# A mixture of experts, three of its eight batches dispatched to tiles of 128 rows

## The chip, the cores and the metric

One core of a Trainium2 chip runs the whole program. The metric is the device time of one execution in microseconds, from the median of several runs.

## The reference, cut to what matters

Four layers follow one another: a delta-rule attention, a mixture of 8 experts with capacity, a gated linear attention with a small two-layer block after it, and last a mixture of 16 experts on tokens with 128 channels, of which each token uses the four most probable. The change is in the last two. With `x` the 4096 tokens (8 batches of 512), the last layer is

```
p = softmax(x @ router_w + router_b)            # 16 experts
w, ids = top_k(p, 4);  w = w / sum(w)
y = sum over k of  w[k] * (gelu(x @ w1[ids[k]] + b1[ids[k]]) @ w2[ids[k]] + b2[ids[k]])
out = x_before + y                              # 128 -> 256 -> 128 channels per expert
```

A token needs 4 of 16 experts. The kernel before computes all 16 for every token, with coefficient 0 for the 12 others.

## The kernel before, in words

All state lies in SBUF. `resid` holds the 4096 tokens as 32 tiles of 128 tokens by 128 channels; `scratch`, cut in blocks of 1024 columns by `carve`, and A1 to A7 hold everything else. The five engines each have one program, written out by hand, and meet by semaphores that count steps (`S(name)`, `at(n)`).

The last mixture runs over units: one unit is one expert on one batch of 512 tokens, 8 x 16 = 128 of them. To be as exact as fp32 with fp16 operands, weights and activations are split into a high and a low fp16 part and three products are added (`PARTS`). A unit goes like this:

- TensorE, `hidden1` (2357): for each of two halves of the 256 hidden channels three matmuls, 128 weights columns wide, over 512 tokens, into one of four PSUM banks. It runs three units ahead (`AHEAD`, 2355).
- ScalarE, `all_experts` (1185): a Gelu per half from PSUM to `h_full` (1191), then one copy to fp16, `h_high` (1195).
- GpSimd (745): the low half, `h_low` = `h_full` - `h_high`, 128 x 1024. TensorE's second layer waits for it (`m1_low`).
- TensorE, `outputs1` (2367): for each of four tiles of 128 tokens six matmuls of 128 columns into bank 4 or 5; it waits for `m1_acc` of two units before.
- VectorE, `accumulate` (1851): four operations, `resid` += coefficient x PSUM (1857).

Beside the units of one batch, the small block and the router of the next batch are worked off in pieces at fixed places of the units' count: normalisation (1738), a transpose, two hidden layers (2280) and an output layer (2296) in split fp16 (in fp32 for batch 0), with VectorE making the low parts (1745, 1750), the addition to `resid` (1755), a second normalisation (1768), a transpose, router logits, softmax and the largest four (1780, 1789), and the coefficients (1803). All these products go through one PSUM bank, bank 6. At the end of each batch the coefficients are transposed (2380) and multiplied with the experts' second biases. GpSimd also makes the low parts of the expert weights (722) and adds terms to `resid` (728). Batches 1 to 6 are run from a loop on TensorE (batches 0 to 6 there) and ScalarE, and written out on VectorE and GpSimd. SP writes each finished batch out.

The second layer of the first mixture in this kernel already scatters rows by indirect DMAs issued from GpSimd (655, 672) and reads them back by DMAs issued from SP (512, 522, 527), combined on VectorE at 1572.

## Time and profile before

| what | us |
|---|---|
| median of 3 runs | 923.57 |
| all three runs | 925.18, 923.51, 923.57 |
| the profiled execution's span, first to last instruction | 921.2 |
| TensorE matmul busy in it | 775.8 (84%), 6152 matmuls |
| VectorE, ScalarE, GpSimd busy in it | 693.3, 628.6, 628.8 |
| mean granted TensorE clock | 0.959 |

The profile is of one execution, and its times are from that execution's first instruction. The last mixture is in it from about 537 us to the end. A matmul's length contains its way through the array, so several overlap; what one costs in a row of them is the distance of the starts. PEld is the load of a matmul's stationary operand, which overlaps the matmuls. In order of time a line merges several instructions of a kind, gives the start and the length from the first start to the last end, and in brackets how long the engine had stood idle and what released it.

### The profile page before, as it was taken

To read this page: it belongs to the slowest core of one execution; us is meant where nothing else is said; L and a number is where in the kernel's file an instruction comes from. 1 tells how busy PE (TensorE), PEld (TensorE's weight loads), DVE (VectorE), ACT (ScalarE), POOL (GpSimd) and SP (SyncE) were. 2 spreads that over 40 slices of the span, in tenths; PEclk is the share of its full clock that TensorE was granted. 3 is DMA by queue.
4 is the path that set the end of the run, shared out by engine and by line. 5 is a ranking of instruction groups with operands and counts; after the bars stand their busy time and mean duration, and the time that the engine had idled before them with its cause. 6 is when DMAs were issued, how large, how long until landed. Compare 5 with 4: busy or idle time off the path is not lost.

```text
span 921.2 us, 18395 instructions
## 1 busy us (share of the span) xinstructions
PE 775.8 (84%) x6152; PEld 470.1 (51%) x6152; DVE 693.3 (75%) x2078; ACT 628.6 (68%) x938; POOL 628.8 (68%) x414
## 2 busy tenths in 40 slices
PE   4965765568998789378778989999999999999997
PEld 1343221124453357223233756777677777677775
DVE  7769799994777578598899878766666666666664
ACT  3855233323455567259788988898888888889895
POOL 4008899730477727466888997686868686868695
PEclk9987889999999799769999999999999999999999
DMA  5999300007200030252600000000000000000000
GB/s 149 119 121 207 113 0 0 15 6 194 87 21 7 4 103 25 82 147 50 202 1 1 1 2 2 12 1 11 0 11 0 12 0 0 11 0 11 0 13 13
DMA packets 52792, 40.47 MB, mean 44 GB/s; under 512 B 6059, under 2 KB 44734, under 8 KB 52734
## 3 DMA queue, kind: packets, MB, share of 16 engines
q1 hardware_dynamic: 49662, 37.28, 18.5%
q0 software_dynamic: 3072, 2.51, 1.0%
q8 instruction: 24, 0.39, 0.2%
q14 instruction: 34, 0.28, 0.1%
HBM read 18.07 MB, written 14.88 MB: 36 GB/s over the span
## 4 chain that ended last, share of the span: by engine, by line
POOL 24%; PE 19%; issue 14%; DVE 14%; ACT 6%; DMA 1%; POOLq 0%; DVEq 0%; ACTq 0%; SPq 0%
POOL scratch L745 21%; PE PS L1909 17%; DVE scratch L1670 2%; DVE resid L1572 2%; DVE stats L1407 1%; DVE scratch L1678 1%; POOL resid L731 1%; PE PS L1916 1%; POOL disp L655 1%; ACT scratch L1195 1%; ACT scratch L1191 1%; DVE resid L1420 1%; DVE A L1432 1%; DVE scratch L1410 1%; ACT A L1126 1%
## 5 line engine op out<-in xcount | busy, mean ns | idle before, releaser
L745 POOL TENSOR_TENSOR scratch<-scratch 128x1024 f16<-128x1024 f32 x128 | 272.9, 2134 | 84.5 <-ACT scratch L1195 82.4
L1857 DVE SCALAR_TENSOR_TENSOR resid<-PS,coef,resid 128x128 f32<-128x128 f32 x512 | 144.0, 344 | 108.9 <-PE PS L1909 103.6
L1909 PEld LDWEIGHTS PS<-A,scratch 128*128 128x128 f16 x3456 | 203.4, 98 | 37.8 <-POOL scratch L745 4.8
L1909 PE MATMUL PS<-A,scratch 128*128 128x128 f16 x3456 | 217.1, 219 | 3.9 <-POOL scratch L745 1.6
L1909 PE MATMUL PS<-A 128*128 (+1 forms) x768 | 186.8, 379 | 0.8 <-DVE A L1701 0.2
L1191 ACT ACTIVATE scratch<-PS,cols 128x512 f32<-128x512 f32 x256 | 163.8, 683 | 25.8 <-PE PS L1909 18.9
L1195 ACT ACTIVATE scratch<-scratch 128x1024 f16<-128x1024 f32 x128 | 135.3, 1057 | 5.0
L1909 PE MATMUL PS<-scratch,ident 128*128 128x512 f32 x160 | 88.3, 673 | 52.9 <-DVE scratch L1373 52.9
L614 POOL TENSOR_TENSOR scratch<-A 128x1024 f32<-128x1024 f32 x32 | 76.0, 2383 | 73.8 <-DVE A L1342 56.5
L1909 PEld LDWEIGHTS PS<-A 128*128 128x128 f16 x768 | 70.7, 98 | 66.6 <-issue 0.6
L655 POOL DMA_INDIRECT disp<-A,scratch x64 | 62.9, 982 | 36.5 <-issue 30.2
L1909 PEld LDWEIGHTS PS<-scratch,ident 128*128 128x128 f32 x160 | 30.7, 209 | 100.2 <-DVE scratch L1373 78.1
L1364 DVE TENSOR_TENSOR_SCAN PS<-PS,scratch 128x512 f32<-128x512 f32 x64 | 74.9, 1215 | 1.9
L1909 PE MATMUL PS<-scratch,A 128*128 128x512 f16 (+1 forms) x216 | 52.8, 390 | 1.4 <-DVE scratch L1520 0.7
L672 POOL DMA_INDIRECT y_rows<-A x32 | 34.2, 1070 | 27.6 <-DVE A L1535 23.6
L1916 PE MATMUL PS<-ident,scratch 128*128 128x128 f32 x128 | 21.4, 294 | 33.4 <-ACT scratch L981 15.5
L694 POOL TENSOR_TENSOR scratch<-scratch,A 128x1024 f32<-128x1024 f32 x16 | 38.3, 2394 | 13.1 <-DVE scratch L1670 4.9
L1909 PE MATMUL PS<-scratch,w_r 128*8 128x512 f32 (+1 forms) x106 | 40.2, 509 | 5.9 <-DVE scratch L1753 3.0
L838 ACT ACTIVATE PS<-A 128x512 f32<-128x512 f32 x33 | 19.7, 599 | 35.8 <-DVE PS L1364 35.8
L683 POOL TENSOR_SCALAR A<-resid,scratch 128x128 f32<-128x128 f32 x32 | 31.3, 989 | 18.5 <-DVE scratch L1584 18.5
L838 ACT ACTIVATE PS<-scratch 128x512 f32<-128x512 f32 x31 | 18.6, 601 | 36.6 <-DVE PS L1364 35.5
L1670 DVE TENSOR_TENSOR_SCAN scratch<-PS,scratch 128x512 f32<-128x512 f32 x32 | 37.3, 1206 | 3.1 <-POOL scratch L694 1.2
(336 smaller groups left out, 1330.9 us busy)
## 6 DMA issues: line engine op xcount, KB each, us to landing
A<-A SPq DMA_DIRECT2D x22, 256.0 KB, 7.4
y_rows<-zeros SPq DMA_DIRECT2D x8, 512.0 KB, 6.0
A<-y_rows SPq DMA_DIRECT2D x14, 256.0 KB, 3.5
disp<-zeros SPq DMA_DIRECT2D x4, 528.0 KB, 21.1
resid<-in_L_attn_x SPq DMA_DIRECT2D x8, 256.0 KB, 4.0
A<-scratch SPq DMA_DIRECT2D x8, 256.0 KB, 6.6
A<-in_L_ffn_ew SPq DMA_DIRECT2D x1, 2048.0 KB, 12.3
A<-scratch SPq DMA_DIRECT2D x32, 64.0 KB, 2.0
```

What stands on the lines that cost most here:

```text
L614: pool.tensor_tensor(c_ring[n % 3], bkR[:, 2 * p:2 * p + 2, :], vR[:, i, :].unsqueeze(1).to_broadcast([128, 2, T]), MUL).then_inc(S("r0_c" ...
L655: pool.indirect_dma_start(out=disp[:, :], in_=rows5[RING_OF[b]][:, k, t, :], in_offset=None, out_offset=bass.IndirectOffsetOnAxis(ap=slot_ ...
L672: pool.indirect_dma_start(out=y_rows[:, :], in_=eo[:, ex * NT + t, :], in_offset=None, out_offset=bass.IndirectOffsetOnAxis(ap=xd[:, ex * ...
L694: pool.tensor_tensor(cbuf[n % 2], cs[n % 2], v1[:, bts(b, T)].unsqueeze(1).to_broadcast([128, 2, T]), MUL).then_inc(S("r_c"), 1)
L745: pool.tensor_tensor(h_low[n % 4], h_full[n % 2], h_high[n % 4], SUB).then_inc(S("m1_low"), 1)
L838: A_(bank(n % 2), kk_pair(a, m)[:, max(i, j) % 2, :], ACT.Identity, scale=-1.0, bias=1.0).then_inc(S("r0_decay"), 1)
L1191: A_(h_full[e % 2][:, h * T:(h + 1) * T], bank((e * HC1 + h) % 4), ACT.Gelu, scale=1.0 / SCALE, bias=cols[:, MB1 + e * HC1 + h:MB1 + e * H ...
L1195: A_(h_high[e % 4], h_full[e % 2], ACT.Copy).then_inc(S("m1_high"), 1)
L1364: V.tensor_tensor_scan(out=bank(2 + 2 * (n % 2) + u), data0=bank(u), data1=c_ring[n % 3][:, u, :], initial=0.0, op0=MUL, op1=ADD).then_inc ...
L1670: last = V.tensor_tensor_scan(out=state[:, j, :], data0=bank(2 + j), data1=cbuf[n % 2][:, j, :], initial=0.0, op0=MUL, op1=ADD)
L1857: last = STT(out=resid[:, g, :], in0=bank(4 + e % 2)[:, t * C:(t + 1) * C], scalar=coef[b % 2][:, t, e:e + 1], in1=resid[:, g, :], op0=MUL ...
L1909: return nc.tensor.matmul(o, l, r, start=start, stop=stop)
```

## The change

Batches 0, 1, 3, 6 and 7 are computed as before, 80 units in all. Batches 2, 4 and 5 are dispatched: each token's row is written four times to a DRAM tensor `disp12`, at the next free place of the region of each of its four experts, and then the regions are worked off in tiles of 128 rows that belong to one expert. Four tiles make a group, which goes through the same steps as a unit. There are always 16 groups: 6144 rows and up to 127 of padding for each expert are at most 63 tiles. In parts:

- The order of units becomes a list: 58 dense units, then eight times one dense unit and two groups, then 14 dense units; 96 in all. Nothing of it is a loop any more.
- The small block and router of the batches start at units `CHAIN_AT` (-2, 6, 13, 20, 27, 31, 44 for batches 1 to 7), alternately in PSUM banks 6 and 7, and the block itself is in fp32, without the split. Small operands of VectorE that lay in bank 7 now lie in SBUF.
- For a dispatched batch: SP copies the row three times, VectorE makes fp16 parts, counts and places, TensorE counts by eight small matmuls, GpSimd issues 16 indirect DMAs (48 in all), and its router logits are in fp32.
- After batch 5 VectorE makes a list of tiles (16 or so small operations), TensorE transposes it, and VectorE writes it as integers to SBUF; SP clears 128 rows behind the last one of each expert (16 DMAs at addresses from registers).
- For each group SP loads four weight addresses to registers and issues four DMAs that copy the experts' first-layer weights (both fp16 parts, 128 x 512 each) from SBUF to a ring of four buffers; it loads four row addresses and issues four DMAs of 128 rows of 528 bytes from `disp12` to a ring of seven. TensorE transposes the rows five units ahead, ScalarE copies them to SBUF.
- The first layer of a group is 32 matmuls of 128 columns (for each half and tile one of 48 rows for the bias and three of 128), the second 28 (one for the bias and six per tile), of which 24 take their weights at a register's address. TensorE loads these registers, four at a time, 16 times, behind dense hidden layers.
- VectorE scales a group's output to a ring of four buffers; GpSimd issues four indirect DMAs that scatter it to DRAM `y12`. At the end SP reads `y12` back in 12 DMAs of 256 KB, and VectorE adds the three batches to `resid`, 16 operations each, after the last three dense units.
- 51 of the 96 low halves are made by VectorE instead of GpSimd: all of the group stretch (units 58 to 85), every other one in units 26 to 54, and a few more.

The core of the diff:

```diff
+        DENSE, SPARSE = (0, 1, 3, 6, 7), (2, 4, 5)
+        CHAIN_AT = (None, -2, 6, 13, 20, 27, 31, 44)
+        GT = 4
+        FIRST_DENSE, LAST_DENSE, COMBINE_BEHIND = 58, 8, 5
+        GROUPS12 = -(-((NS * T * TOP1 + E1 * 127) // 128) // GT)
+        left = [("dense", i, e) for i in range(ND) for e in range(E1)]
+        UNITS = [left.pop(0) for _ in range(FIRST_DENSE)]
+        for g in range(GROUPS12):
+            if g % 2 == 0 and len(left) > LAST_DENSE:
+                UNITS.append(left.pop(0))
+            UNITS.append(("group", g, 0))
+        UNITS += left
+        AHEAD, TR_AHEAD, SCATTER_BEHIND = 3, 5, 3
+        XT_RING, YO_RING, XG_RING = 7, 4, 3
+        SCATTER_AT = [CHAIN_AT[b] + 20 for b in SPARSE]
+        LOW_BY_DVE = set(SCATTERS) | {a + 1 for a in CHAIN_AT[2:]} | set(range(SCATTER_AT[NS - 1], SCATTER_AT[NS - 1] + 8))
+        LOW_BY_DVE |= set(range(UNIT_OF_GROUP[0] - 1, UNIT_OF_GROUP[-1] + 5))
...
+            for g in range(GROUPS12):
+                if g >= XT_RING:
+                    n = g - XT_RING
+                    sp.wait_ge(*since(s_yo[n % YO_RING], 16 * GT * (n // YO_RING + 1)))
+                if g >= WT_RING:
+                    sp.wait_ge(S("m1_hid_mm"), at(2 * UNIT_OF_GROUP[g - WT_RING] + 1))
+                columns = registers(mybir.EngineType.SP, tile_list[:, GT * g:GT * g + GT], (E1 - 1) * HC1 * 128)
+                for t, w in enumerate(columns):
+                    sp.dma_start(wt[g % WT_RING][:, t, :, :], w1_hl[:, :, bass.ds(w, HC1 * 128)]).then_inc(s_xt[g % XT_RING][0], 16)
+                first_row = registers(mybir.EngineType.SP, tile_list[:, 128 + GT * g:128 + GT * g + GT], NOBODY)
+                for t, r in enumerate(first_row):
+                    sp.dma_start(xt[g % XT_RING][:, t, :], disp12[bass.ds(r, 128), :]).then_inc(s_xt[g % XT_RING][0], 16)
...
+            def scatter_outputs(g):
+                pool.wait_ge(S("m1_acc"), at(UNIT_OF_GROUP[g]))
+                pool.wait_ge(*since(s_xt[g % XT_RING], 32 * GT * (g // XT_RING + 1)))
+                for t in range(GT):
+                    pool.indirect_dma_start(out=y12[:, :], in_=yo[g % YO_RING][:, t, :], in_offset=None,
...
+            def evict(u, g):
+                dve.wait_ge(S("m1_out_mm"), at(u))
+                if g >= YO_RING:
+                    dve.wait_ge(*since(s_yo[g % YO_RING], 16 * GT * (g // YO_RING)))
+                TS(yo[g % YO_RING], bank(4 + u % 2).rearrange("p (n c) -> p n c", c=C), 1.0 / SCALE, None,
+                   MUL).then_inc(S("m1_acc"), 1)
+            def low_half(u):
+                dve.wait_ge(S("m1_high"), at(u))
+                dve.wait_ge(S("m1_out_mm"), at(u, 4))
+                TT(h_low[u % 4], h_full[u % 2], h_high[u % 4], SUB).then_inc(S("m1_low_dve"), 1)
...
+            for u in range(NU):
+                kind, i, e = UNITS[u]
+                if u + 2 < NU and not LOW_BY_POOL[u + 2]:
+                    low_half(u + 2)
+                if kind == "dense":
+                    accumulate(u, i, e)
+                else:
+                    evict(u, i)
...
             def hidden11(c, h):
-                for k, (sw, sx) in enumerate(PARTS):
-                    last = mm(bank(6), tile(u1_hl[:, sw, :], h), hT11_hl[:, sx, :], start=k == 0, stop=k == len(PARTS) - 1)
+                pe.wait_ge(S("xT_copied"), 3 * B + at(c))
+                chain_bank_read(c)
+                mm(chain_bank(c), tile(u_1, h), hT11).then_inc(S("hid11_mm"), 1)
...
+                for h in range(HC1):
+                    pe.wait_ge(S("m1_hid"), at(2 * u + h, 4))
+                    for t in range(GT):
+                        out = tile(bank((2 * u + h) % 4), t)
+                        mm(out, mb1_hl[:, h * 128:h * 128 + 128], picked_expert(i, t), stop=False)
+                        for k, (sw, sx) in enumerate(PARTS):
+                            last = mm(out, wt[i % WT_RING][:, t, sw, h * 128:h * 128 + 128], tile(x, sx * GT + t), start=False,
+                                      stop=k == len(PARTS) - 1)
...
+                        mm(out, picked_expert(i, t), mb2_hl, stop=False)
+                        for h in range(HC1):
+                            for k, (sw, sh) in enumerate(PARTS):
+                                part = (h_high, h_low)[sh][u % 4][:, h * T + t * 128:h * T + t * 128 + 128]
+                                last = mm(out, part, w2_hl[:, sw, bass.ds(weights_at[i][t] + h * 128, 128)], start=False,
+                                          stop=k == len(PARTS) - 1 and h == HC1 - 1)
...
-            with pe.Fori(0, B - 1) as b:
-                all_experts(b, False)
-            all_experts(B - 1, True)
+            for u in range(NU):
+                if u + AHEAD < NU:
+                    hidden1(u + AHEAD)
+                outputs1(u)
...
+                if u == LIST_AT:
+                    list_transposed()
+                if u + TR_AHEAD < NU and UNITS[u + TR_AHEAD][0] == "group":
+                    group_transposed(UNITS[u + TR_AHEAD][1])
```

## Rows read from the trace of the kernel before

**Rows 1.** The page: TensorE in 40 slices; line 745's group (busy, mean ns, idle)

```profile
PE   4965765568998789378778989999999999999997
...
L745 POOL TENSOR_TENSOR scratch<-scratch 128x1024 f16<-128x1024 f32 x128 | 272.9, 2134 | 84.5 <-ACT scratch L1195 82.4
```

**Rows 2.** Stretches of a whole batch and of the last: busy us by engine

```profile
692.00:740.00 48.00, 47.64 (x545) 34.69 (x543) 33.06 (x130) 42.60 (x58) 36.73 (x19) 1.00 0.02 6
...
870.00:912.00 42.00, 42.00 (x488) 30.88 (x486) 23.05 (x94) 38.54 (x51) 33.17 (x16) 1.00 0.03 8
```

**Rows 3.** TensorE in order of time, last batch (start us, length us)

```profile
875.87 1.46 PE L1909 MATMUL PS<-A 128*128 128x512 f16 x6
...
877.16 1.50 PE L1909 MATMUL PS<-A,scratch 128*128 128x128 f16 x24
...
907.49 1.46 PE L1909 MATMUL PS<-A 128*128 128x512 f16 x6
```

**Rows 4.** TensorE in order of time, a batch run from the loop

```profile
675.17 0.50 PE L1909 MATMUL PS<-coef,A 128*128 128x16 f16 x12
...
675.74 1.46 PE L1909 MATMUL PS<-A 128*128 x6
...
681.54 0.40 PE L1909 MATMUL PS<-coef,scratch 48*128 48x128 f16 x4
...
681.87 1.47 PE L1909 MATMUL PS<-A 128*128 x6
...
699.41 0.82 PE L1909 MATMUL PS<-scratch,w_r 128*128 128x512 f16 x3 [0.32 <-DVE scratch L1753]
...
705.41 0.28 PE L1909 MATMUL PS<-w_v,scratch 128*128 128x128 f16 x2
...
706.76 1.46 PE L1909 MATMUL PS<-A 128*128 x6
...
723.01 0.52 PE L1909 MATMUL PS<-coef,A 128*128 128x16 f16 x12
```

**Rows 5.** TensorE in order of time, the fp32 block of batch 0

```profile
515.88 1.12 PE L1909 MATMUL PS<-scratch,u 128*128 128x512 f32 x2
...
516.84 1.05 PE L1909 MATMUL PS<-u_o,A 128*128 128x128 f32 x8
...
519.68 2.05 PE L1909 MATMUL PS<-u,scratch 128*128 128x128 f32 x16
...
521.57 1.06 PE L1909 MATMUL PS<-ident,scratch 128*128 128x128 f32 x8
...
528.49 0.46 PE L1909 MATMUL PS<-coef,A 128*128 128x16 f16 x12 [0.90 <-DVE A L1774]
```

**Rows 6.** TensorE in order of time, a wait for the splits of batch 1

```profile
561.97 0.28 PE L1909 MATMUL PS<-w_v,scratch 128*128 128x128 f16 x2 [1.08 <-DVE scratch L1753]
```

**Rows 7.** ScalarE in order of time: the step from TensorE's end

```profile
710.24 1.33 ACT L1191 ACTIVATE scratch<-PS,cols 128x512 f32<-128x512 f32 x2 [0.21 <-PE PS L1909]
```

**Rows 8.** VectorE in order of time: single operations

```profile
387.80 2.44 DVE L1572 SCALAR_TENSOR_TENSOR resid<-A,scratch,resid 128x128 f32<-128x128 f32 x8 [6.96 <-DMA A<-y_rows]
...
507.25 1.22 DVE L1678 TENSOR_TENSOR scratch<-PS,scratch 128x1024 f32<-128x1024 f32 x1
...
697.94 0.69 DVE L1752 CAST scratch<-PS 128x512 f16<-128x512 f32 x1 [0.32 <-ACT PS L1138]
...
915.41 1.12 DVE L1857 SCALAR_TENSOR_TENSOR resid<-PS,coef,resid 128x128 f32<-128x128 f32 x4
```

**Rows 9.** GpSimd in order of time: an indirect DMA

```profile
381.55 0.97 POOL L672 DMA_INDIRECT y_rows<-A  x1 [0.30 <-issue]
```

**Rows 10.** SP's queue in order of time: issues of 128 and 256 KB

```profile
385.09 1.90 SPq L522 DMA_DIRECT2D A<-y_rows  x4
...
387.03 5.03 SPq L527 DMA_DIRECT2D A<-y_rows  x6
```

**Rows 11.** The page's DMA issues: KB each, median us to landing

```profile
A<-scratch SPq DMA_DIRECT2D x32, 64.0 KB, 2.0
```

More of the change, by code:

```diff
@@ L348, in build, with chain_bank, low_made @@
+        carry12, region12 = sm[:, 480:496], sm[:, 496:512]
+        def chain_bank(c):
+            return bank(6 + c % 2)
+        def low_made(u):
+            n = sum(p == LOW_BY_POOL[u] for p in LOW_BY_POOL[:u])
+            return (S("m1_low"), at(n)) if LOW_BY_POOL[u] else after("m1_low_dve", n)
         h_full = [carve(n) for n in range(2)]
@@ L409, in build, with registers @@
         fetched = [v[:, :].rearrange("p (n c) -> p n c", c=C) for v in (A6, A7)]
+        def registers(engine, values, most):
+            return nc.values_load_multi_w_load_instructions(
+                values, engines=[engine], min_val=0, max_val=most,
+                skip_runtime_bounds_check_because="made on VectorE from counts that add up to the rows")[1]
         block = ctx.enter_context(nc.Block())
@@ new lines, in _ @@
+            copy_rows(0)
+            written_out(DENSE[0], LAST_UNIT[0])
+            copy_rows(1)
+            written_out(DENSE[1], LAST_UNIT[1])
+            copy_rows(2)
+            sp.wait_ge(*after("tiles_listed", 0))
+            for k in range(E1 // 4):
+                first_free = registers(mybir.EngineType.SP, tail_row[:, 4 * k:4 * k + 4], NOBODY - 128)
+                for r in first_free:
+                    sp.dma_start(disp12[bass.ds(r, 128), :], zeros[:, :]).then_inc(s_tail[0], 16)
@@ L546, in _ @@
+            written_out(DENSE[4], LAST_UNIT[4])
+            for i in range(NS):
+                sp.wait_ge(*after("y_combined", i))
+                sp.dma_start(ov[SPARSE[i]], resid[:, bts(SPARSE[i], NT), :]).then_inc(s_out, 16)
             sp.wait_ge(s_out, X_LAST + 16 * B)
@@ new lines, in _ @@
+            for u in range(NU):
+                if LOW_BY_POOL[u]:
+                    low_half(u)
+                if u in (1, 2):
+                    low_weights(B - 3 + u)
+                for c in range(2, B):
+                    if u == CHAIN_AT[c]:
+                        add_up(c)
+                for i in range(NS):
+                    if u == max(SCATTER_AT[i] - 10, 3):
+                        token_ids(i)
+                for i, n in SCATTERS.get(u, ()):
+                    scatter_tokens(i, n)
+                if u >= SCATTER_BEHIND and UNITS[u - SCATTER_BEHIND][0] == "group":
+                    scatter_outputs(UNITS[u - SCATTER_BEHIND][1])
@@ L1903, in _ @@
+            for i in range(max(0, LAST_DENSE - COMBINE_BEHIND), NS):
+                combine12(i)
             dve.drain().then_inc(stage_done, 1)
@@ L2318, in logits12 @@
             def logits12(c):
-                pe.wait_ge(S("x_low"), at(c))
+                if c in SPARSE:
+                    pe.wait_ge(*after("xT12_copied", sparse_of(c)))
+                else:
+                    pe.wait_ge(S("x_low"), at(dense_of(c)))
+                chain_bank_read(c)
                 for t in range(NT):
+                    logits = chain_bank(c)[:, t * E1:(t + 1) * E1]
+                    if c in SPARSE:
+                        last = mm(logits, tile(A3[:, bts(c, T)], t), u_r[:, :])
+                        continue
@@ L2352, in _ @@
             pe.wait_ge(S("w_low"), at(1))
[L2355 to L2364 removed]
+            weights_at = {}
@@ L2374, in outputs1 @@
                             w = slice((e * HC1 + h) * 128, (e * HC1 + h) * 128 + 128)
-                            part = (h_high, h_low)[sh][e % 4][:, h * T + t * 128:h * T + t * 128 + 128]
-                            last = mm(tile(bank(4 + e % 2), t), part, w2_hl[:, sw, w],
-                                      start=k == 0 and h == 0, stop=k == len(PARTS) - 1 and h == HC1 - 1)
+                            part = (h_high, h_low)[sh][u % 4][:, h * T + t * 128:h * T + t * 128 + 128]
+                            last = mm(out, part, w2_hl[:, sw, w], start=k == 0 and h == 0,
+                                      stop=k == len(PARTS) - 1 and h == HC1 - 1)
@@ L2418, in _, with list_transposed @@
+            def list_transposed():
+                pe.wait_ge(*after("tile_values", 0))
+                chain_bank_read(0)
+                for k in range(2):
+                    mm(bank(6)[0:1, 128 * k:128 * k + 128], tile_values[:, k:k + 1], ident[:, :])
+                last = mm(bank(6)[0:3 * E1, 256:384], tile_expert, ident[:, :])
+                last.then_inc(S("tiles_mm"), 1)
+                read_by[0] = after("tiles_listed", 0)
+            hidden1(0)
             project1(5)
-            hidden1(0, 1)
+            hidden1(1)
```

666 lines of the change are left out of this document (447 added, 219 removed).

## The prediction, made before the changed kernel was run

> **What bounds the kernel now.** I read the page first, then the stretches of the last mixture, then TensorE's order of time in it. The page [rows 1] shows where it is: from the 23rd slice on TensorE is busy 9 tenths at full clock and hardly any DMA runs. The stretch of one whole batch, and that of the last one [rows 2], separate the engines: TensorE 47.64 of 48 us and 42.00 of 42, ScalarE 42.60 and 38.54, GpSimd 36.73, VectorE 33.06. The chain of waits names GpSimd's line 745 most, but GpSimd idles 84.5 us before those 128 steps [rows 1], so TensorE decides. Its order of time in the last batch [rows 3] gives the unit that I count in: one expert on one batch is six matmuls of 512 columns (1.29 us) and 24 of 128 columns (1.34 us), 2.635 us in all (12 units from 875.87 to 907.49; six matmuls from 875.87 to 877.16). Batches 1 to 6 run from the loop at the same pace, so unrolling it is worth nothing. The block before the mixture for the next batch takes what 16 units leave of the 47.84 us from a batch's router matmuls to the next one's (675.17 to 723.01), 5.7 us, with one wait of 0.32 for VectorE's splitting [rows 4].
>
> **Part 1, dense units removed.** 128 units become 80: 48 x 2.635 = **-126.5 us**.
>
> **Part 2, groups added.** 3 x 512 x 4 rows plus the padding bound are 63 tiles, so 16 groups of four, whatever the routing is. A group is 32 first-layer and 28 second-layer matmuls and 8 transposes, all of 128 columns. Rows 3 give 1.34 / 24 = 0.0558 us for a weight load and matmul of that size; 68 x 0.0558 = 3.79. Twelve of them have 48 rows; the four 48-row ones of today take 0.33 us [rows 4], 0.083 each, so +0.33. That is 4.12 x 16 = **+66 us**. A register in an address costs nearly nothing: the 12 small router matmuls, addressed by the loop's register, take 0.57 us from 675.17 to 675.74 [rows 4] against 0.46 busy for those of batch 0 [rows 5], under 10 ns each.
> The Trainium skill, "TensorE: Matmul & The Clock Gate", section "Back-to-back issue gap", says that a sustained stream of weight load and 128-column matmul runs at about 81 ns each. By that 68 would take 5.5 us; this trace has 55.8 ns for the stream, and I follow the trace.
>
> **Part 3, the block before the mixture, fp32.** Its two hidden layers go from three 512-column fp16 matmuls, 0.65, to one fp32 one, 0.96 us each (515.88 to 516.84), its output layer from 1.35 (705.41 to 706.76) to 1.89 (519.68 to 521.57) [rows 4, 5]: 1.16 more, x7 = 8.1. Sparse batches lose the coefficients' transposes and the bias product (0.66) and gain the counts (8 tiny matmuls, about 0.4); their router logits, 4 fp32 matmuls of 16 columns for 12 fp16 ones, I leave at 0.57. With the list of tiles: **+8.5**. The waits for the splits go: 0.32 x 6 [rows 4], and two of 1.08 beside batch 0, one shown [rows 6], of which some come back as a wait for batch 2's normalisation: **-3**.
> TensorE's own work thus falls by 52 us. The rest is what this newly meets.
>
> **Part 4, VectorE in units 26 to 47.** The chains of batches 4, 5, 6 start 7, 7 and 4 units apart instead of 16, and VectorE takes 13 of these 22 units' low halves. Today it has no such row; the nearest of its own is 1.22 us for 128x1024 from PSUM and SBUF [rows 8], the farthest is GpSimd's 2.13 for the same work [rows 1]. I take 1.22, the same engine's, with bounds 0.7 (a 512-column fp16 write takes 0.69 [rows 8]) and 2.13. VectorE: accumulations 22 x 1.05, low halves 13 x 1.22, three chains and a third of 13.2 each, tile list 3.6 (some 17 small dependent operations of 0.2): 86. The 13.2: of the 33.06 busy us of a batch [rows 2] 16 x 1.12 are accumulations, five splits of 0.7 go, 11.7 are left, and gaps between dependent operations and the placing of rows add 1.5. TensorE: 22 x 2.635 + 3.3 x 5.5 = 76. The surplus lands in TensorE's waits for `m1_low_dve`, `m1_acc` and the tile list: **+10** (4 with the slack of two units, 23 with low halves of 2.13).
>
> **Part 5, the first group.** GpSimd has 26 scatters left after unit 43; each takes 0.97 + 0.30 [rows 9], 33 us, then 2.0 to land [rows 11]. Only then may SP load registers, issue 8 DMAs at 0.475 (four in 1.90) [rows 10] and have them land in 2.0: 42 to 43 us. TensorE needs the rows at the end of unit 54, 39 us of its own work later, up to 5 more by part 4. **+4** (0 to 10).
>
> **Part 6, register loads.** On TensorE 16 loads of four values, two at a time, stand in the queue between hidden and output layers, and both layers wait behind them. No row shows one. Below: nothing, if the six matmuls queued ahead (1.3 us) cover a pair. Above: 2.0 us, the landing of a small DMA [rows 11], 32 us in all. I take the nearest round trip in rows, the 0.2 us from TensorE's end to ScalarE's start [rows 7], times four, 0.8 us; with a third covered, **+8** (0 to 32).
> The Trainium skill, "DMA: Bandwidth & Descriptors", section "Latency and other measured facts", states a floor of about 600 ns for a tensor load; 16 of them would be 9.6 us. No run here shows one yet.
>
> **Part 7, supply of the groups.** SP per group: 8 issues x 0.475 + 2 loads x 0.8 = 5.4 us. GpSimd: 4 scatters, 5.1. TensorE: (2.635 + 2 x 4.12)/2 + its loads, about 6. Bytes: 0.5 MB weights, 0.26 MB rows, 0.26 MB out, 1.03 MB; six transfers of 256 KB were issued in 5.03 us [rows 10], 305 GB/s, so 3.4 us. ScalarE: two units and copies about 3.3. All fit under 6, with little room; the seven-deep row ring closes on itself (fetch 8, five units 18, output and evict 5, scatter and landing 7 = 38 us, 5.4 per group). **+4** (0 to 35, below). GpSimd is free of low halves there, so a late scatter harms SP's wait alone, and through it the next rows.
>
> **Part 8, the end.** Three combinations of 16 operations each, 1.04 per four in a row (as accumulations from PSUM; eight of the kind took 2.44 with a wait between [rows 8]), 4.2 each, stand in VectorE's queue after units 93, 94 and 95. Those units have no hidden layer left, so TensorE ends 2.7 after unit 93; VectorE needs 3 x 1.05 + 12.6. It ends 13 after TensorE instead of with one accumulation of 1.12 [rows 8]: **+12**. Their rows are in SBUF by then, scattered 14 dense units earlier. The last write out is of the same size as now. The 3 extra loads at the start (under 0.5 each on SP) and the smaller set-up are covered by loads and products not on the path: 0, at worst 1.4.
>
> **Sum.** -126.5 + 66 + 8.5 - 3 + 10 + 4 + 8 + 4 + 12 = -17. The profiled execution's span is 921.2; the median of the runs is 923.57, 2.4 above it, which I keep. 921.2 - 17 + 2.4 = **906.6 us**.
>
> **Rivals.**
> *Supply-bound groups (slower).* Place: SP's loop over groups, with rings of 7, 4 and 4 behind it. For: `y_rows` transfers issued with a full queue took 0.84 each over six [rows 10]. With 0.84, SP needs 8.3 us per group, 2.3 over TensorE's 6 for 15 groups: +35, **941**. It decides from 7.1 us per group, reached also if one load of four takes 1.65 us. Against: those six were twice to four times larger. Chance 0.2, times from 925 up.
> *No overlap of load and matmul.* If in groups, where 48-row and 128-row operands alternate, every pair took the 0.083 of today's 48-row ones [rows 4], 16 x 56 x 0.027 = +24: 931. All dense rows speak against. Chance 0.03.
> The sentence of the Trainium skill on 81 ns ("TensorE: Matmul & The Clock Gate", above) describes this case.
> *VectorE at GpSimd's pace.* Low halves of 2.13: +13, **920**, as SBUF reads of both fp32 operands could be slower than PSUM's. Chance 0.1.
> *Cheap extras.* Register loads covered, the surplus absorbed, supply in time: -8 - 6 - 4 - 2 = **887**. For it: TensorE's queue had no gap in 30 us of rows 3. Chance 0.25.
> *It does not shrink the work*, if routing filled more tiles: excluded, the count of groups is fixed in the code.
> *Forecast*, 898 to 918: chance 0.42.
>
> **Chances and range.** A measurement of this kernel can tell about 0.2%, 1.8 us. Faster: forecast 0.42, cheap 0.25, most of the VectorE case 0.05: 0.72. Within 0.2%: 0.05. Slower: 0.23. The likeliest sign's own range is 886 to 920; to hold 8 in 10 the top takes in most of the supply case: 886 to 938.
>
> **What would show it.** Dense units at 2.635 and groups at 4.1 on TensorE's order of time; waits of TensorE for VectorE's low half and accumulation around 650 to 720; one wait of some us for the first rows; gaps after every third dense hidden layer by register loads; SP's issues in groups of 5 to 6 us; VectorE alone for 13 us at the end. The forecast is wrong if group units are spaced 7 us or more, if the waits for `xt` recur for each group, or if VectorE's low half is near 2 us.

## The result, and the profile of the changed kernel

The changed kernel takes 993.34 us (988.68 to 994.37) against 923.57 before: ratio 1.0735, interval 1.0697 to 1.0774. The forecast was 906.6, range 886 to 938. The profiled execution has a span of 992.6 us at a mean granted clock of 0.922 (before 921.2 at 0.959). Each ratio below is to the kernel before measured beside that kernel; it took 923.6 to 924.9 us, but twice 945.9 and 951.9, and a time from beside those two is compared with no other.

The page, the lines that answer to [rows 1]: the span, TensorE in 40 slices, and the low halves on GpSimd (45 instead of 128).

```profile
span 992.6 us, 17478 instructions
...
PE   5866555689997892887788679779786969999993
...
L899 POOL TENSOR_TENSOR scratch<-scratch 128x1024 f16<-128x1024 f32 x45 | 97.9, 2179 | 88.2 <-ACT scratch L1403 87.5
```

From the 22nd slice to the 33rd TensorE has no run of nines any more, in the very stretch in which it was to have work without gaps. What it waits for from 530 us on (waits of TensorE: us in total, times, longest):

```profile
PE PS L2238 <- DVE scratch L1957: 19.3, 7, 5.9
PE PS L2231 <- DVE resid L2123: 14.2, 8, 5.3
PE PS L2774 <- DMA A<-disp: 8.8, 2, 8.4
```

Line 1957 is the normalisation ahead of a chain, 2123 the accumulation. An accumulation takes no longer than before (1.13 us for four), so the question is what stood ahead of it in VectorE's queue, which is worked off in order. VectorE in order of time (start us, length us) ahead of the 5.3 us wait for line 2123:

```profile
563.04 2.12 DVE L1948 TENSOR_SCALAR scratch<-scratch 128x8 f32<-128x8 f32 x1
565.19 0.17 DVE L1949 TENSOR_SCALAR scratch<-scratch 128x8 int32<-128x8 int32 x1
565.40 0.17 DVE L1951 TENSOR_TENSOR scratch<-scratch 128x8 f32<-128x8 f32 x1
565.60 2.08 DVE L1952 TENSOR_TENSOR scratch<-scratch 128x8 f32<-128x8 f32 x1
567.71 0.17 DVE L1953 SCALAR_TENSOR_TENSOR scratch<-scratch 128x8 f32<-128x8 f32 x1
```

GpSimd in order of time beside it:

```profile
563.00 2.12 POOL L899 TENSOR_TENSOR scratch<-scratch 128x1024 f16<-128x1024 f32 x1
565.52 4.37 POOL L899 TENSOR_TENSOR scratch<-scratch 128x1024 f16<-128x1024 f32 x2 [0.40 <-ACT scratch L1403]
```

Operations on 4 or 8 numbers per partition take 2.1 us, and they end with GpSimd's: 563.04 + 2.12 = 565.16, and GpSimd's ends at 563.00 + 2.12 = 565.12. Between two of GpSimd's operations they take 0.17. The diff's one line `P7 = carve(8)[:, 0:512]` moved these operands from a PSUM bank to SBUF. This is the first cause (tested below). The first second-layer block of the mixture comes at 557.92 instead of 537.34, before any dense unit is saved.

The second cause is in the groups. TensorE in order of time, one quarter of a hidden bank and one of an output bank:

```profile
844.31 0.23 PE L2231 MATMUL PS<-nr,mb_hl 48*128 48x128 f16 x1
844.47 0.34 PE L2231 MATMUL PS<-A 128*128 128x128 f16 x3
844.74 0.23 PE L2231 MATMUL PS<-nr,mb_hl 48*128 48x128 f16 x1
...
847.94 0.23 PE L2231 MATMUL PS<-coef,nr 48*128 48x128 f16 x1
848.10 0.51 PE L2231 MATMUL PS<-A,scratch 128*128 x6
848.54 0.23 PE L2231 MATMUL PS<-coef,nr 48*128 48x128 f16 x1
```

From start to start a bias matmul of 48 rows and three of 128 take 0.435 us, four of 128 rows would take 0.223 [rows 3]; one and six take 0.60 instead of 0.39. With eight of the first, four of the second and the transposes, 0.45 to 0.54, a group takes 6.4 us, not 4.12.

A wait costs more than its length. In the 4 us behind the wait of 5.34 that ends at 574.07 the granted clock is 0.50, the lower of TensorE's two levels, 1.2 GHz, and 24 matmuls of 128 columns take 2.51 us (574.07 to 576.58) instead of 1.34; the six matmuls of 512 columns behind them take 2.17 (576.58 to 578.75) instead of 1.29, so this wait costs another 2.05 us. 4 us later the clock is 0.98. Windows of all engines (us; busy us of PE, PEld, DVE, ACT, POOL; granted clock; DMA share, GB/s):

```profile
574.00:578.00 4.00, 3.93 (x28) 3.14 (x29) 3.90 (x20) 0.00 (x0) 1.27 (x1) 0.50 0.01 4
578.00:586.00 8.00, 8.00 (x83) 6.06 (x82) 7.48 (x41) 4.76 (x6) 0.73 (x1) 0.98 0.00 0
```

### The profile page after: what moved, and what is told of

Its sections match the earlier page's. It is cut to its first block and busy times, and to the rows that moved or that the text cites. A ratio compares the mean times of both kernels' runs of the same rounds, so it can differ in the third digit from the quotient of the medians.

```text
span 992.6 us, 17478 instructions
## 1 busy us (share of the span) xinstructions
PE 780.5 (79%) x5724; PEld 462.6 (47%) x5724; DVE 743.0 (75%) x1998; ACT 570.4 (57%) x856; POOL 583.3 (59%) x445
## 5 line engine op out<-in xcount | busy, mean ns | idle before, releaser
L2231 PE MATMUL PS<-A,scratch 128*128 128x128 f16 (+1 forms) x2688 | 182.3, 223 | 16.5 <-DVE resid L2123 14.2
L2231 PEld LDWEIGHTS PS<-A,scratch 128*128 128x128 f16 x2688 | 161.5, 100 | 44.9 <-issue 21.3
L2231 PE MATMUL PS<-A 128*128 128x512 f16 (+1 forms) x864 | 169.3, 322 | 0.1
L899 POOL TENSOR_TENSOR scratch<-scratch 128x1024 f16<-128x1024 f32 x45 | 97.9, 2179 | 88.2 <-ACT scratch L1403 87.5
L2123 DVE SCALAR_TENSOR_TENSOR resid<-PS,coef,resid 128x128 f32<-128x128 f32 x320 | 89.9, 343 | 73.7 <-PE PS L2231 67.9
L1396 ACT ACTIVATE scratch<-PS,cols 128x512 f32<-128x512 f32 x160 | 101.7, 685 | 67.1 <-DVE scratch L2137 35.4
L810 POOL DMA_INDIRECT disp<-A,scratch x64 | 62.9, 982 | 36.7 <-issue 30.3
L913 POOL DMA_INDIRECT disp<-A,scratch x48 | 57.7, 1203 | 20.5 <-issue 12.1
L921 POOL DMA_INDIRECT y<-scratch,A x32 | 35.7, 1116 | 50.3 <-DVE scratch L2131 43.0
L2137 DVE TENSOR_TENSOR scratch<-scratch 128x1024 f16<-128x1024 f32 x51 | 62.1, 1218 | 0.3
L921 POOL DMA_INDIRECT y<-A x32 | 36.6, 1145 | 22.3 <-DVE A L2131 13.5
L2238 PEld LDWEIGHTS PS<-ident,scratch 128*128 128x128 f32 x128 | 16.6, 160 | 68.5 <-issue 42.8
```

The lines of the kernel that those rows point to most:

```text
L810: pool.indirect_dma_start(out=disp[:, :], in_=rows5[RING_OF[b]][:, k, t, :], in_offset=None, out_offset=bass.IndirectOffsetOnAxis(ap=slot_ ...
L899: pool.tensor_tensor(h_low[u % 4], h_full[u % 2], h_high[u % 4], SUB).then_inc(S("m1_low"), 1)
L913: pool.indirect_dma_start(out=disp12[:, :], in_=rows12[i][:, k, t, :], in_offset=None, out_offset=bass.IndirectOffsetOnAxis(ap=slot12[i][: ...
L921: pool.indirect_dma_start(out=y12[:, :], in_=yo[g % YO_RING][:, t, :], in_offset=None, out_offset=bass.IndirectOffsetOnAxis(ap=xt[g % XT_R ...
L1396: A_(h_full[u % 2][:, h * T:(h + 1) * T], bank((2 * u + h) % 4), ACT.Gelu, scale=1.0 / SCALE, bias=cols[:, MB1 + e * HC1 + h:MB1 + e * HC1 ...
L2123: last = STT(out=resid[:, g, :], in0=bank(4 + u % 2)[:, t * C:(t + 1) * C], scalar=coef[i % 2][:, t, e:e + 1], in1=resid[:, g, :], op0=MUL ...
```

## The experiments

All but the first start from the changed kernel. Four marks of TensorE's order of time separate their stages: the first second-layer block of the mixture, the first group's transposes, TensorE's end, the span (us). They are of the profiled execution, which is up to 3.3 us off the median of its kernel; gains are taken from the medians.

| kernel | first block | first group | TensorE ends | span |
|---|---|---|---|---|
| before | 537.3 | – | 915.2 | 921.2 |
| changed | 557.9 | 808.1 | 975.8 | 992.6 |
| small operands in PSUM | 543.0 | 766.4 | 934.3 | 951.2 |
| 128-row biases | 555.2 | 799.1 | 949.5 | 966.3 |
| both | 542.7 | 764.9 | 918.9 | 935.7 |
| both, weights in place | 543.1 | 761.9 | 906.2 | 923.0 |
| and low halves on VectorE | 545.7 | 764.4 | 900.3 | 917.1 |
| and 60 units ahead | 543.5 | 764.5 | 894.3 | 911.1 |

**Small operands in SBUF, in the kernel before.**

```diff
-        P7 = bank(7)
+        P7 = carve(8)[:, 0:512]
```

> The kernel before with one edit: the small operands of the normalisations and of the router move from PSUM bank 7 to the SBUF slot that the change gives them; order and work are as before. Theory A (in the changed kernel VectorE's small operations with all operands in SBUF are held up while GpSimd runs a TENSOR_TENSOR; there four of 128x128 took 4.33 and 4.43 us instead of 1.12): 15 to 25 us slower than before, most of it ahead of the first second-layer block (537.34 in the kernel before, 557.92 in the changed one), since behind it each chain has 16 units of slack; normalisations of 128x128 with means well over 0.3 us. Rival (the lateness comes from the changed order of the queues, the place of the operands is harmless): within 2 us of before.

Measured: 1039.59 us, ratio 1.1246 (1.1227 to 1.1265): 115 us slower by this one line. The place of the operands alone does it. The size was far off, and so was its place: the first second-layer block comes at 551.7, 14.4 us late, and 100 us are lost behind it. I had counted on the 16 units of slack of each chain, but VectorE's queue is in order and every accumulation stands behind the small operations: TensorE waited 66.7 us in 14 pieces for accumulations (first row). In this kernel GpSimd makes all 128 low halves. Most small operations still take 0.16 us (the median of line 1728), since one of GpSimd's holds up one of VectorE's and the next few go through before GpSimd starts again; but most chains of them are caught several times, for up to 2.0 us. Waits, then VectorE's lines (duration min/median/max in ns) of this kernel:

```profile
PE PS L1909 <- DVE resid L1857: 66.7, 14, 6.9
...
L1787 DVE TENSOR_TENSOR scratch<-scratch x8: 224/1177/1182, 537.9 to 976.1; 128x64 f32<-128x64 f32 x8
L1728 DVE TENSOR_TENSOR scratch<-scratch x24: 161/163/2007, 589.0 to 962.2; 128x4 f32<-128x4 f32 x21, 128x24 f32<-128x24 f32 x3
L1786 DVE TENSOR_REDUCE scratch<-scratch x8: 220/220/221, 537.6 to 975.8; 128x4 f32<-128x64 f32 x8
L1857 DVE SCALAR_TENSOR_TENSOR resid<-PS,coef,resid x512: 330/343/353, 559.7 to 1031.1; 128x128 f32<-128x128 f32 x171
```

And two of the same lines in the kernel before, operands in PSUM:

```profile
L1787 DVE TENSOR_TENSOR PS<-PS,scratch x7: 232/232/232, 581.3 to 868.3; 128x64 f32<-128x64 f32 x7
L1728 DVE TENSOR_TENSOR PS<-PS,scratch x24: 170/170/191, 567.6 to 855.8; 128x4 f32<-128x4 f32 x21, 128x24 f32<-128x24 f32 x3
```

The operation that reads two tensors in SBUF is held up; the reduction, with one, never is (221 ns at most), nor the accumulation, whose first operand is in PSUM (353). That is the rule of the Trainium skill, "SBUF — State Buffer", section "Who interferes with whom": a VectorE instruction with two SBUF inputs contends with a GpSimd instruction that reads SBUF, since its second input comes over a read interface that the two share. The same section lets casts and TENSOR_SCALAR contend with one input too, in a mode of two ports; line 1948 above took 2.12 us with one input, so the trace agrees.

**Small operands back in PSUM, in the changed kernel.** The logits and exponentials, which ScalarE shares, stay in SBUF; the bank comes from the hidden layers' ring.

```diff
-        P7 = carve(8)[:, 0:512]
+        P7, P8 = bank(7), carve(8)[:, 0:512]   # lg_P, exp_P in P8
-            return bank(6 + c % 2)
+            return bank(3 if c % 2 else 6)
-    bank((2 * u + h) % 4)  ...  at(2 * u + h, 4)
+    bank((2 * u + h) % 3)  ...  at(2 * u + h, 3)
```

> The changed kernel with the small operands back in PSUM bank 7, all but the logits and their exponentials, which ScalarE shares; the banks for it come from a ring of three hidden banks instead of four. Theory A: 30 to 50 us faster than the changed kernel, about 20 of it ahead of the first second-layer block and the rest from TensorE's waits for VectorE behind it (41 us between 558 and 767 in the changed kernel). Rival B (VectorE is overloaded by chains that start 7 units apart and by its 51 low halves): under 10 us behind that block, the waits for accumulations and low halves stay. A ring of three that is too short would show as new waits of TensorE for ScalarE's line of the hidden layers.

Measured: 953.34 us (1.0312; 1.0293 to 1.0331), 40.0 faster than the changed kernel: 14.9 ahead of the first block, where I expected about 20, 26.8 in the stretch up to the first group, nothing behind it (table). Of the first block's lateness 5.7 us stay (543.0 against 537.3), with one wait of 3.8 for a normalisation among them. The waits for accumulations are gone, those for normalisations fall from 19.3 to 9.0 us; the shorter ring costs 4.0 us of new waits for line 1396:

```profile
PE PS L2238 <- DVE scratch L1957: 9.0, 5, 3.8
...
PE PS L2231 <- ACT scratch L1396: 4.0, 5, 1.3
```

Theory A holds for most of it. What rival B names is left: 15 waits from 568 to 726, 21.9 us together, for VectorE or for a step of ScalarE; 3.0 of them are for line 1396 and so may belong to the shorter ring.

**Nearly all low halves on VectorE**, small operands still in SBUF, so that GpSimd has only short TENSOR_TENSORs left (1.27 us, 512 columns).

```diff
-        LOW_BY_POOL = [u not in LOW_BY_DVE for u in range(NU)]
+        LOW_BY_POOL = [u < 2 for u in range(NU)]
```

> The changed kernel with the low halves of all units but the first two on VectorE, so that GpSimd has hardly a TENSOR_TENSOR left in the last mixture; the small operands stay in SBUF. Theory A (GpSimd's TENSOR_TENSOR holds up VectorE's operations that have all operands in SBUF): behind the first units the small operations take 0.16 to 0.23 us and a normalisation 0.35 throughout, where the changed kernel has maxima of 2.0 to 2.3; TensorE's waits for normalisations fall to a third, while 43 more low halves of 1.22 us make VectorE the bound elsewhere, so the time itself may go either way by 20 us. Rival (the small operations are slow in SBUF for another reason, such as their own dependences): the maxima stay near 2 us.

Measured: the hold shrinks to what GpSimd still runs, it does not vanish, so the maxima stayed above the 0.35 expected: 1.19 and 1.12 us on lines 1951 and 1952 (2.28 and 2.08 in the changed kernel), but 1.98 on line 1953. VectorE in order of time:

```profile
581.92 1.19 DVE L1951 TENSOR_TENSOR scratch<-scratch 128x8 f32<-128x8 f32 x1
583.14 0.17 DVE L1952 TENSOR_TENSOR scratch<-scratch 128x8 f32<-128x8 f32 x1
```

GpSimd beside it:

```profile
581.82 1.26 POOL L887 TENSOR_TENSOR resid<-resid,A 128x512 f32<-128x512 f32 x1
```

581.92 + 1.19 = 583.11, GpSimd's 581.82 + 1.26 = 583.08: it is GpSimd's operation that sets the length, here 1.2 us instead of 2.1. The one of 1.98 us, at 752.88, ends like the others with a TENSOR_TENSOR of GpSimd's (754.86 against 753.54 + 1.28 = 754.82), but begins 0.66 ahead of it, beside the issue of a scatter; what held it so early is open. The rival (their own dependences) would have kept the 2 us throughout. TensorE's waits for normalisations did not fall to a third: from 530 us on they are 21.2 us, against 19.3. The time, 1051.24 us, was measured beside a kernel before of 945.9 and is compared with nothing.

**Bias matmuls in groups of four.**

```diff
+                    for t in range(GT):
+                        mm(tile(bank(...), t), mb1_hl[...], picked_expert(i, t), start=t == 0, stop=False)
                     for t in range(GT):
-                        mm(out, mb1_hl[...], picked_expert(i, t), stop=False)
                         for k, (sw, sx) in enumerate(PARTS):
```

(and alike in the second layer; the last of the bank alone has `stop`)

> The changed kernel with the bias matmuls of a group unit (48 rows) issued four in a row ahead of the 12 or 24 matmuls of 128 rows, as one accumulation group per bank; same instructions, same count. In the changed kernel a bias matmul and three others take 0.435 us, where four of 128 rows take 0.223. Theory C1 (each change between 48 and 128 rows costs about 0.21 us): changes fall from 12 to 3 pairs per group, 16 x 9 x 0.21 = 30 us faster, a hidden bank 1.1 us instead of 1.74. Theory C2 (each 48-row or broadcast operand costs it, whatever stands beside it): within 3 us of the changed kernel.

**Bias operands of 128 rows**, the rows from 48 on zero.

```diff
-        mb1_hl = sb("mb1_hl", [3 * E1, HC1 * 128], f16)
+        mb1_rows = sb("mb1_hl", [128, HC1 * 128], f16)   # and mb2_rows, set to 0 first
-        tile_picks = late[0:3 * E1, 64:128].bitcast(f16)
+        tile_picks = late[:, 64:128].bitcast(f16)
```

> The changed kernel with the bias operands of the groups padded by zero rows to 128; broadcast operand, register addresses, order and count stay. Theory C (the row count is what costs): 192 x 0.21 = 40 us faster, a bias matmul and three others 0.223 us, a group 3.9 us; the supply of rows and weights may then show as waits for the groups' DMAs and take some of it back. Rival (the broadcast operand or the address from a register costs): within 3 us of the changed kernel.

Measured: 976.09 us (1.0563; 1.0543 to 1.0583), 17.3 faster than the changed kernel, and 968.37 (1.0474; 1.0457 to 1.0492), 25.0 faster. TensorE in order of time, four in a row and then 12, in the first:

```profile
812.76 0.40 PE L2231 MATMUL PS<-nr,mb_hl 48*128 48x128 f16 x4
813.09 0.84 PE L2231 MATMUL PS<-A 128*128 128x128 f16 x12
813.87 0.40 PE L2231 MATMUL PS<-nr,mb_hl 48*128 48x128 f16 x4
```

and padded rows in the second:

```profile
806.76 0.22 PE L2236 MATMUL PS<-nr,mb_hl 128*128 128x128 f16 x1
806.82 0.33 PE L2236 MATMUL PS<-A 128*128 128x128 f16 x3
806.99 0.22 PE L2236 MATMUL PS<-nr,mb_hl 128*128 128x128 f16 x1
```

A hidden bank takes 1.11 us grouped (813.87 - 812.76) against 1.74, and a padded quarter 0.223 to 0.23 against 0.435. The operand is broadcast and picked per tile in both, so it is not that; the same count of 48-row matmuls costs less when they stand together, so it is the alternation. Each change to 48 rows and back costs 0.21 us: C1, not C2.

The totals fell short of 30 and 40 us, though, and longer waits for the groups' rows make up more than half of what is missing: 8.8 us in 2 pieces became 15.9 in 8 and, in the second,

```profile
PE PS L2779 <- DMA A<-disp: 18.3, 9, 5.0
```

SP's queue in that kernel, in order of time, weight copies (L689) and row loads (L692) of a group by turns:

```profile
792.09 2.90 SPq L689 DMA_DIRECT2D A<-A  x4
795.53 1.95 SPq L692 DMA_DIRECT2D A<-disp  x4
797.95 2.86 SPq L689 DMA_DIRECT2D A<-A  x4
801.35 3.22 SPq L692 DMA_DIRECT2D A<-disp  x4
805.03 2.86 SPq L689 DMA_DIRECT2D A<-A  x4
```

12.94 us for two groups (792.09 to 805.03), 6.5 per group; a weight copy takes 0.72 to issue, not 0.475. TensorE alone would need 5.4 per group, (2.635 + 2 x 3.9 + 0.45) / 2.

**Both.**

> The changed kernel with both mends: small operands in PSUM, bias operands of 128 rows. If the two causes are separate, the gains add: 993.3 - 40.0 - 25.0 = 928 us. If they share a part (both only shift the point from which the supply of groups decides), the sum of the gains is smaller, 935 us or more. Supply theory: TensorE's waits for the groups' rows stay at 15 to 20 us, since SP needs 6.3 us per group (four weight copies at 0.72, four row loads at 0.48, 1.0 for the register loads) and TensorE (2.63 + 2 x 3.9 + 0.45)/2 = 5.4.

Measured: 935.74 us (1.012; 1.009 to 1.0149), 57.6 faster than the changed kernel: less than the sum of the two gains, 65.0, as expected for causes that share a part. The shared part is the supply: the rows are waited for 24.2 us in 9 pieces.

**Both, and the first layer's weights in place.**

```diff
-  mm(out, wt[i % WT_RING][:, t, sw, h * 128:h * 128 + 128], tile(x, sx * GT + t), ...)
+  mm(out, w1_hl[:, sw, bass.ds(weights_at[i][t] + h * 128, 128)], tile(x, sx * GT + t), ...)
-                for t, w in enumerate(columns):
-                    sp.dma_start(wt[g % WT_RING][:, t, :, :], w1_hl[:, :, bass.ds(w, HC1 * 128)])...
```

> As the one with both mends, and the first layer too takes its weights in place, by the address register that the second layer has anyway; the 64 weight copies are left out. Supply theory (SP's issue of eight DMAs per group bounds the groups): SP then needs under 3 us per group, the waits for the groups' rows fall from about 18 us to the first group's wait alone (5 to 9), 8 to 12 us faster than with both mends. Rival (the rows themselves or the ring behind the scatters are late, the copies were free): within 3 us of the one with both mends. Second rival: a matmul whose weights' address comes from a register costs more than 0.056 us; it would show in the row of the first layer.

Measured: 924.80 us (1.0016; 1.0002 to 1.003), 10.9 faster, as the supply theory says. TensorE's waits from 530 us on:

```profile
PE PS L2231 <- ACT scratch L1396: 10.5, 6, 6.5
...
PE PS L2774 <- DMA A<-disp: 4.6, 1, 4.6
```

Only the first group's wait for rows is left. The first row has grown from 7.2 us: its longest piece, 6.5 us, is at 882, where GpSimd comes from its last scatter to the low halves at 879.25. An address from a register costs nothing in the first layer either (0.056 per matmul as before).

The changed kernel with this edit alone:

> The changed kernel with one edit: the first layer of a group takes its weights in place by the address register, the 64 weight copies are left out. Theory (in the changed kernel the supply is hidden behind groups of 6.4 us, only the first group's wait holds SP's eight issues): within 1 to 5 us faster than the changed kernel, and the groups stay at 6.4 us. Rival (the copies themselves, by their issues or their traffic, slow the groups): 10 us faster or more.

Measured: 1035.74 us beside a kernel before of 945.9, and a second time 1059.52 beside 951.9. Neither can be set against 993.34, so whether the copies cost anything in the changed kernel is not settled by a time; in the changed kernel's trace rows are waited for at the first two groups only, 8.4 and 0.5 us.

**Combinations earlier**, at 7, 5 and 3 units before the end, and then **61 units ahead**.

```diff
-                n = u - NU + LAST_DENSE - COMBINE_BEHIND
-                if 0 <= n < NS:
-                    combine12(n)
+                if u - NU in (-7, -5, -3):
+                    combine12((u - NU + 7) // 2)
...
-        FIRST_DENSE, LAST_DENSE, COMBINE_BEHIND = 58, 8, 5
+        FIRST_DENSE, LAST_DENSE, COMBINE_BEHIND = 61, 8, 5
```

> As the one with weights in place, and the three combinations stand in VectorE's queue 7, 5 and 3 units before the end instead of 3, 2 and 1. Theory (the end is VectorE's own work of 3 x 4.7 us behind TensorE's last matmul): VectorE idles 1.5 us per unit before that, and the rows have landed by then, so 3 to 5 us faster. Rival (the rows land too late for it, or TensorE falls behind by waits for accumulations): no gain.

> As the one with early combinations, and the first group comes after 61 dense units instead of 58, so that 11 instead of 14 dense units stand behind the last group. Theory (the first group waits 9 us of TensorE's time for GpSimd's scatters and the loads behind them): 3 x 2.63 = 7.9 us of that wait are filled, 3 x 1.5 come back at the end, where VectorE has less time for the combinations: 2 to 5 us faster. Rival (what the groups wait for is bound to the units' order too): no gain or slower.

Measured: 931.31 us (1.0074; 1.0053 to 1.0094), 6.5 slower than without, and 928.62 (1.0047; 1.0034 to 1.0061). The first is the rival, and its reason is the first cause again. At 897.71 VectorE took up the first combination and was done with it at 909.3, 11.6 us for work of 4.7; the two outputs behind it held up TensorE for 7.3 us. The rows were not late: VectorE waits for no DMA there, and SP had issued the last of the 12 loads by 891.7. But a combination has both tensor operands in SBUF, and here GpSimd still makes low halves. VectorE's line, then two of its 16 operations, and GpSimd in order of time:

```profile
L2152 DVE SCALAR_TENSOR_TENSOR resid<-A,scratch,resid x16: 337/342/2293, 897.7 to 909.0; 128x128 f32<-128x128 f32 x16
...
899.91 2.22 DVE L2152 SCALAR_TENSOR_TENSOR resid<-A,scratch,resid 128x128 f32<-128x128 f32 x1
...
902.43 2.29 DVE L2152 SCALAR_TENSOR_TENSOR resid<-A,scratch,resid 128x128 f32<-128x128 f32 x1
```

```profile
899.82 2.16 POOL L899 TENSOR_TENSOR scratch<-scratch 128x1024 f16<-128x1024 f32 x1 [0.51 <-ACT scratch L1403]
902.45 2.12 POOL L899 TENSOR_TENSOR scratch<-scratch 128x1024 f16<-128x1024 f32 x1 [0.47 <-ACT scratch L1403]
```

Four of the 16 take 1.75 to 2.29 us instead of 0.34 and end 0.15 behind GpSimd's; that is 7.0 us, all of the 11.6 - 4.7. At the end of the changed kernel, where GpSimd has done its last low half, the same 16 take 4.7. With 61 units ahead 2.7 us are gained back.

**Low halves of four more units on VectorE**, combinations as in the changed kernel.

```diff
-  LOW_BY_DVE |= set(range(UNIT_OF_GROUP[0] - 1, UNIT_OF_GROUP[-1] + 5))
+  LOW_BY_DVE |= set(range(UNIT_OF_GROUP[0] - 1, UNIT_OF_GROUP[-1] + 9))
```

> The kernel with both mends, weights in place and four more low halves on VectorE, a third time, since in both calls before the kernel before took 946 and 952 us. Theory (the 6.5 us wait at 882 behind GpSimd's last scatter goes): where the kernel before takes 924 us, 918 to 920. Rival: the combinations' rows decide the end, 924 to 926. If the kernel before again takes over 940, the ratio says what the long unrolled mixture costs in that state, about 1.045.

Measured: 915.57 us (0.9911; 0.9893 to 0.9929), 8.1 below the kernel before; the wait at 882 is gone, of 10.5 us for line 1396 3.3 are left. By the medians, which were not measured side by side, that is 9.2 below the 924.80 without it, by the spans 5.9, where 5 to 7 were expected. Beside the kernel before of 945.9 and 951.9 it took 985.11 and 996.81.

**60 units ahead.**

```diff
-        FIRST_DENSE, LAST_DENSE, COMBINE_BEHIND = 58, 8, 5
+        FIRST_DENSE, LAST_DENSE, COMBINE_BEHIND = 60, 8, 5
```

> The kernel with both mends, weights in place and four more low halves on VectorE (915.6 us), with the first group after 60 dense units instead of 58. Theory (TensorE's wait for the first group's rows, 4.6 us, can be filled with two units of 2.64): 2 to 4 us faster, 912 to 914. Rival (two units fewer stand behind the groups, so the rows for the combinations land later than VectorE is ready, and GpSimd and VectorE meet the same work later): 915 to 918.

Measured: 913.23 us (0.9879; 0.986 to 0.9898), beside 924.92 for the kernel before. No wait for rows is left among TensorE's. The 2.3 us gained are what the theory gave, but they are not clear of noise: the intervals of the two ratios, 0.986 to 0.9898 and 0.9893 to 0.9929, overlap. Beside the kernel before of 945.9 and 951.9 this one took 990.78 and 1001.32, no gain over 58 units.

A version with the chain of batch 6 two units later, meant to thin out VectorE's work where two chains overlap, computed wrong values, so its 1005.54 us say nothing, and what is left for VectorE stays untested.

## Why the prediction was wrong, by its own steps

**The step that is missing: the move of the small operands.** The prediction costs the parts of the change one by one, and the line that moves `P7` from a PSUM bank to SBUF is in none of them. It took the chain's 11.7 us of VectorE per batch, part 4, from rows with the operands in PSUM [rows 2]. With most of them moved back (and a hidden ring shorter by one bank for it) the kernel is 40.0 us faster, so this is at least 40 of the 86.7 us between 993.34 and the forecast of 906.6.

**Part 2, groups, +66: mis-sized.** 6.4 us measured against 4.12, 16 x 2.3 = +37. The twelve 48-row matmuls were priced by four that stand together, 0.083 [rows 4]; among 128-row ones each costs 0.265. The rival "no overlap" named the right place, the alternation, and priced it by the same row: 0.027 on each of 56, where it is 0.21 on each of 12. The row of its price showed one change per four. The kernel before already showed it, in a line just ahead of the one I used: the 24 matmuls before those four take 1.43 us to the next start (681.54 - 680.11) instead of 1.34. With the 0.33 - 0.22 of the four themselves that is 0.20 for one change.

TensorE in order of time, kernel before:

```profile
680.11 1.50 PE L1909 MATMUL PS<-A,scratch 128*128 128x128 f16 x24
```

With the rows padded the stream ran at 0.0558 a matmul, as the sum had it. The Trainium skill, "TensorE: Matmul & The Clock Gate", section "Back-to-back issue gap", has 81 ns; that did not show, not even in the groups.

**Part 7, supply, +4, and its rival (941).** SP needs 6.4 to 6.5 us per group instead of 5.4, since a weight copy from SBUF to SBUF takes 0.72 to issue where I had priced it by loads of the same 128 KB from DRAM, 0.475 [rows 10]. In the changed kernel groups of 6.4 hide this, 7.7 us of TensorE for each with its share of a dense unit, so the term is 0; with the groups at their forecast pace it is the rival's mechanism, worth the 10.9 us that the weights in place gave. It bites below the rival's 7.1 us, as TensorE, without a cost for register loads, needs 5.4 and not 6.

**Part 4, VectorE's surplus, +10: near.** With the small operands mended 21.9 us of waits for VectorE, directly or through ScalarE, are left. 13.9 of them, with the 3.0 for line 1396, lie in the stretch that the part is about, from 650 us on, where I had 10; the 8.0 ahead of it were in no term. There, with both mends and the weights in place, VectorE has no gap from 650 to 667 us, where two chains overlap. The low halves took 1.22 as assumed (51 of them, mean 1218 ns).

**Part 6, register loads, +8: nothing.** Between the last dense hidden block and its output block there is no gap where four values are loaded. TensorE in order of time, changed kernel:

```profile
825.43 1.46 PE L2231 MATMUL PS<-A 128*128 128x512 f16 x6
826.73 1.50 PE L2231 MATMUL PS<-A,scratch 128*128 128x128 f16 x24
828.07 0.61 PE L2774 MATMUL PS<-coef,A 128*128 128x128 f16 x8
```

1.30 from the first start to the second, as without loads, and none of TensorE's waits in the mixture is without a releaser. The Trainium skill, "DMA: Bandwidth & Descriptors", section "Latency and other measured facts", states 600 ns for a tensor load; no run here shows them on TensorE's time, covered as they are.

**Part 5, the first group, +4:** 8.4 us, within its 0 to 10.

**Part 8, the end, +12:** right. TensorE's last block ends at 975.8, VectorE's last combination at 985.24 + 4.66 = 989.9, 14.1 later instead of 13. VectorE in order of time:

```profile
985.24 4.66 DVE L2152 SCALAR_TENSOR_TENSOR resid<-A,scratch,resid 128x128 f32<-128x128 f32 x16
```

**Part 3** held as far as looked at: the two hidden layers in fp32 took 0.92 each, an output layer 1.84. **Part 1** held: dense units are 2.635 apart. (Of the slices in [rows 1] from the 23rd on, the 24th shows 8 tenths and not 9; nothing rests on it.)

**The slower clock** was in no term. From 535 us on the mean granted clock is 0.92, where the kernel before has 1.00, and the one wait followed above cost 2 us more behind it. The two steps above and the supply together are worth 68.5 of the 86.7 us (993.34 - 924.80); how the rest divides between the clock and the waits was not separated.

The forecast of a gain was wrong even for the mended change: with its two flaws and the supply mended it takes 924.80, the time of the kernel before (1.0016) and 18.2 above the forecast. Only with four more low halves moved and the first group two units later does it come to 913.23, 1.2% below the kernel before; that is another kernel than the one forecast, and coming within 6.6 of the 906.6 does not bear out the sum.

## What to carry to other kernels

When a diff moves an operand between PSUM and SBUF, look for who else reads SBUF at that time: a VectorE operation with two tensor operands in SBUF (a TENSOR_SCALAR even with one) costs its own time, 0.17 us for a small one and 0.34 for 128x128, or lasts until GpSimd's current TENSOR_TENSOR ends, and what stands behind it in the queue pays. Price an operation from a row in which its neighbours are the same, not only its shape: a 48-row matmul costs 0.083 us as one of four in a row and 0.265 alone between 128-row ones. And a mend may only uncover the next bound, so read the waits again after each.

## What the runs showed that was not expected

Twice the kernel before took 945.9 and 951.9 us instead of 924, the first time on a chip that had also given 924.8, and beside it the changed kernels, with the mixture unrolled, lost more: the version with four more low halves on VectorE, 0.9911 of the kernel before otherwise, was 1.0426 and 1.0489 of it. TensorE's waits in its trace beside 945.9 have a row that is absent from its trace at 915.57:

```profile
PE PS L2231 <- issue: 28.7, 51, 1.5
```

51 stops in which it waited for nothing that the profile shows. That the supply of instructions is behind it, which a loop needs less of, is only argued; the kernel before has no trace from there.

Rows are not the only shape whose change costs. In the changed kernel four transposes of the coefficients, whose stationary operand has 128 rows and 48 columns, follow six matmuls of 128 by 128, and from 849.30 to 850.07 the ten take 0.77 us instead of 0.56: the same 0.21. No experiment varied this.
